# Three one-pass products for the local attention's projections, and a quantised layer whose mask TensorE adds

## What is computed

```python
def local_attention(x, Wq, Wk, Wv, Wo):     # 32 heads of 16, window 128
    q, k, v = heads(x @ Wq.T), heads(x @ Wk.T), heads(x @ Wv.T)
    scores = einsum('bhnrd,bhncd->bhnrc', blocks(q), two_blocks(k)) / sqrt(16)
    probs = softmax(where(valid, scores, min))
    return heads_joined(einsum('bhnrc,bhncd->bhnrd', probs, two_blocks(v))) @ Wo.T

def quantised(x, weight, bias):             # bias: [4, 1, 512]
    x_dq = float8_e4m3(clip(x * s, -448, 448)) / s      # s = 448 / max|x|
    w_dq = ...                                          # the same of weight
    return einsum('bmk,bkn->bmn', x_dq, w_dq) + bias

x = layernorm(x + local_attention(x, ...))
x = layernorm(x + quantised(x, ctx, mask))
```

## Time and profile before

| | us |
|---|---|
| median of 3 runs | 2390.05 |
| lowest, highest run | 2386.92, 2391.8 |
| span of the profiled execution, first to last instruction | 2399.8 |
| of it the local attention, from its first to its last stretch | 987.2 to 1499.5 |
| of it the quantised layer | 1500.2 to 1564.9 |

### The profile page before, as it was taken

One profiled execution on the slowest core, in us unless ns is written; L12 is line 12 of the kernel. 1 busy time (PEld: TensorE's weight loads), 2 busy tenths in 40 slices (PEclk: granted clock), 3 DMA queues, 4 the chain that ended last, 5 costly groups with the idle time before them and its releaser, 6 DMA issues. The chain is left out here.

```text
span 2399.8 us, 30995 instructions
## 1 busy us (share of the span) xinstructions
PE 2155.6 (90%) x10708; PEld 1150.3 (48%) x10711; DVE 1360.3 (57%) x3183; ACT 799.9 (33%) x1325; POOL 680.1 (28%) x944
## 2 busy tenths in 40 slices
PE   9999979989999999889999987478888888889994
PEld 5777748754444444344444443233333333336762
DVE  5866768856212217376667674945656565445443
ACT  5554624420122121233434332523323222123333
POOL 1300015526323320333343333011113121214553
PEclk9999989979999999999999998689999999999997
DMA  7211232270177754444333420300000000066555
GB/s 261 79 36 53 88 127 75 93 287 1 58 236 244 256 172 147 132 100 94 80 84 79 96 52 1 113 3 1 2 19 2 19 28 19 18 172 163 101 98 167
DMA packets 101672, 231.31 MB, mean 96 GB/s; under 512 B 18886, under 2 KB 42614, under 8 KB 94366
## 3 DMA queue, kind: packets, MB, share of 16 engines
q1 hardware_dynamic: 78974, 187.64, 25.2%
q0 software_dynamic: 22560, 41.87, 7.9%
HBM read 170.49 MB, written 63.53 MB: 98 GB/s over the span
## 5 line engine op out<-in xcount | busy, mean ns | idle before, releaser
L2083 DVE CUSTOM_DVE_ANT_0 D_ps<-D_ps,D_mask 128x256 f32<-128x256 f32 (+1 forms) x512 | 186.8, 420 | 68.5 <-PE D_ps L1980 67.4
L1832 POOL TENSOR_SCALAR_AFFINE_SELECT D_probs<-D_probs 128x256 f32<-128x256 f32 x256 | 106.6, 422 | 284.1 <-ACT D_probs L1890 283.8
L1890 ACT ACTIVATE D_probs<-D_ps 128x512 f32<-128x512 f32 (+1 forms) x256 | 125.3, 542 | 163.9 <-PE D_ps L2002 163.9
L3082 DVE TENSOR_REDUCE F_neg_max<-F_ps 128x4 f32<-128x2048 f32 (+1 forms) x64 | 93.9, 1489 | 109.7 <-PE F_ps L2980 103.6
L2832 ACT ACTIVATE F_probs<-F_ps 128x1536 f32<-128x1536 f32 (+1 forms) x48 | 76.4, 1591 | 189.8 <-PE F_ps L2996 189.8
L1393 PE MATMUL C_ps<-C_down_shared,C_hs 128*128 128x512 f32 x256 | 115.4, 600 | 1.9 <-DVE C_hs L1560 1.9
L1381 PE MATMUL C_ps<-C_xT,C_gate_shared 128*128 128x512 f32 x256 | 115.4, 593 | 0.5 <-ACT C_xT L1256 0.5
L1381 PE MATMUL C_ps<-C_xT,C_up_shared 128*128 128x512 f32 x256 | 115.1, 592 | 0.0
L1980 PE MATMUL D_ps<-D_k_stack,D_q_stack 96*128 96x256 bf16 (+1 forms) x512 | 92.6, 266 | 8.9 <-DVE D_maxima L2083 7.3
L1230 POOL DMA_INDIRECT expert_sums<-C_y,C_of_slot x32 | 50.3, 1571 | 173.5 <-ACT C_y L1297 102.2
L2713 POOL TENSOR_SCALAR_AFFINE_SELECT F_probs<-F_probs 128x512 f32<-128x512 f32 x64 | 41.1, 654 | 181.9 <-ACT F_probs L2832 181.9
(11 more groups left out here) (549 smaller groups left out, 4878.9 us busy)
## 6 DMA issues: line engine op xcount, KB each, us to landing
C_ring<-moe_experts_dram SPq DMA_DIRECT2D x32, 1536.0 KB, 7.2
qk_parts<-D_parts SPq DMA_DIRECT2D x32, 384.0 KB, 2.5
expert_sums<-A_zeros SPq DMA_DIRECT2D x1, 8192.0 KB
C_ring<-expert_sums SPq DMA_DIRECT2D x5, 1536.0 KB, 10.0
D_q_stack<-qk_parts SPq DMA_DIRECT2D x16, 384.0 KB, 4.9
...
```

The costliest lines, as they stand in the source:

```text
L1832: last = nc.gpsimd.affine_select(now[:, :, 0:P], now[:, :, 0:P], [[0, 2], [1, P]], ALU.is_ge, 0.0, base=0, channel_multiplier=-1)
L1890: nc.scalar.activation(probs[at % 2][:, 2 * pair:2 * pair + 2, 0:w], ps[:, 4 + unit % 3, :].rearrange("p (h q) -> p h q", h=2)[:, :, 0:w], ...
L2083: last = nc.vector.tensor_tensor_reduce(now, now, mask[:, first:256], 1.0, -3e38, ALU.add, ALU.max, maxima[n % 2][:, head, t:t + 1])
L3082: last = nc.vector.tensor_reduce(neg_max[n % 2][:, :, t], ps[:, 0:GROUP, at:at + w], AX_X, ALU.max, negate=True)
```

## The change

In the attention `x`, `Wq`, `Wk` and `Wv` are each split in a high part, rounded to a one-pass format (F32R), and the rest, and a projection or value piece becomes three one-pass products, high by high, high by low and low by high: 12 instructions per job for 8. ACT casts the high parts (`keep_xT`, `high_of`), DVE subtracts the low ones (`low_xT`, `low_of`). Pieces are spread over the half-slots by a cost in us. To make room, the stacks hold three chunks, the rest of a split one buffer, and rows of v are packed at 17 per head.

In the quantised layer the clip is fused into the rounding addition, the mask is scaled, split in three bfloat16 rows and added by one more matmul per tile, and the means are taken once per batch.

```diff
@@ window_attention_layer: the plan of the fillers
+    PIECES = {"turn_x": 1, "turn_o": 1, "project": 3 * KD, "values": 3 * KD, "out": KD}
+    COST = {"turn_x": 0.44, "turn_o": 0.44, "project": 0.23, "values": 0.23, "out": 0.86}
...
-        pieces = [(kind, n, k) for kind, n in jobs_of(i) for k in range(1 if kind.startswith("turn") else KD)]
+        pieces = [(kind, n, k) for kind, n in jobs_of(i) for k in range(PIECES[kind])]
...
+        costs = [COST[piece[0]] if piece else COST["out"] for piece in pieces]
+        least = 2 * SLOTS * (COST["out"] if i >= CHUNKS else 3 * COST["project"])
+        total, spent = max(sum(costs), least), 0.0
         for at in range(2 * SLOTS):
-            many = max(len(pieces), 2 * SLOTS)
-            now = [piece for piece in pieces[at * many // (2 * SLOTS):(at + 1) * many // (2 * SLOTS)] if piece]
+            now = []
+            while pieces and (at == 2 * SLOTS - 1 or spent + costs[0] / 2 <= (at + 1) * total / (2 * SLOTS)):
+                spent += costs.pop(0)
+                now.append(pieces.pop(0))
@@ tensors
-        xT = sb("xT", [P, KD, S])
+        xT_hi, xT_lo = sb("xT_hi", [P, KD, S], F32R), sb("xT_lo", [P, KD, S], F32R)
-        rest = [sb(f"rest{j}", [P, S]) for j in (0, 1)]
-        q_stack, k_stack = sb("q_stack", [STACK + 3, HEADS, S], BF16), sb("k_stack", [STACK + 3, HEADS, S], BF16)
-        v = [sb(f"v{j}", [P, 4, HEADS, 2 * DK]) for j in (0, 1)]
+        rest = sb("rest", [P, S])
+        q_stack, k_stack = (sb(n, [STACK + 3, RING_D * HC, S], BF16) for n in ("q_stack", "k_stack"))
+        v = [sb(f"v{j}", [P, 4, V_ROW]) for j in (0, 1)]
...
+        evicted = {"turn_x": xT_lo_ready, "project": rest_ready, "values": v_ready, "turn_o": oT_ready, "out": summed}
@@ SyncE
             def restack(m):
+                n, c = m // 2, m // 2 % RING_D
+                if n >= RING_D:
+                    sp.wait_ge(scoresT_ready, 2 * SLOTS * (n - RING_D + 1))
@@ ScalarE
+            for n in range(4):
+                keep_xT(n)
+            for k in range(KD):
+                high_of(wq_hi[:, k, :], wq[:, k, :], wq_in[k], wq_hi_ready)
+            high_of(wk_hi[:], wk[:], wk_in, wk_hi_ready)
...
+                if i == FIRST + 1:
+                    high_of(wv_hi[:], wv[:], wv_in, wv_hi_ready)
@@ TensorE, a piece of a projection (values alike)
+                    part, q = divmod(k, KD)
...
+                    if k == KD:
+                        pe.wait_ge(xT_lo_ready, 4 * (n // 8 + 1))
+                    if k == 2 * KD:
+                        pe.wait_ge(wk_lo_ready if n % 2 else wq_lo_ready, 1)
-                    last = nc.tensor.matmul(ps[:, bank, :], w[:, k, c * P:(c + 1) * P], xT[:, k, :], start=(k == 0), stop=(k == KD - 1))
+                    last = nc.tensor.matmul(ps[:, bank, :], (w_lo if part == 2 else w_hi)[:, q, c * P:(c + 1) * P],
+                                            (xT_lo if part == 1 else xT_hi)[:, q, :], start=(k == 0), stop=(k == 3 * KD - 1))
@@ VectorE
             def split(m):
-                if m >= 2:
-                    dve.wait_ge(mid_ready, m - 1)
+                if m >= 1:
+                    dve.wait_ge(lo_ready, m)
...
+            def low_xT(n):
+                dve.wait_ge(xT_ready, n + 1)
...
+                nc.vector.tensor_tensor(xT_lo[:, :, now], ps[:, number["turn_x", n] % 2, :].rearrange("p (k m) -> p k m", k=KD),
+                                        xT_hi[:, :, now].bitcast(F32), ALU.subtract).then_inc(xT_lo_ready, 1)
+            def low_of(w_lo, w, w_hi, w_hi_ready, count, w_lo_ready):
+                dve.wait_ge(w_hi_ready, count)
+                nc.vector.tensor_tensor(w_lo, w[:], w_hi[:].bitcast(F32), ALU.subtract).then_inc(w_lo_ready, 1)
...
+                        for kind, n in done(i, at, 0, "turn_x"):
+                            if n >= 4:
+                                low_xT(n)
@@ fp8_layer, SyncE
-            for b in range(B):
-                sp.dma_start(mask[:, b, :], d["mask"][b].partition_broadcast(P)).then_inc(mask_in, 16)
+            sp.dma_start(mask[:], d["mask"]).then_inc(mask_in, 16)
...
+            for z, part_ready in enumerate((mask_hi_ready, mask_mid_ready, mask_lo_ready)):
+                sp.wait_ge(part_ready, 1)
+                sp.dma_start(mask_rows[z:z + 32 * (B - 1) + 1:32, :], mask_parts[z][:]).then_inc(mask_stacked, 16)
             load_constants(sp)
@@ ScalarE
             def deviations(b):
+                act.wait_ge(mean_ready, b + 1)
                 for t in range(b * 4, b * 4 + 4):
-                    act.wait_ge(mean_ready, t + 1)
@@ TensorE
+                    nc.tensor.matmul(ps[:, t, :], ones[32 * b:32 * b + 3, :], mask_rows[32 * b:32 * b + 3, :], start=False,
+                                     stop=True).then_inc(out_ready, 1)
@@ VectorE
-                steps.after(nc.vector.tensor_scalar(w[:], w[:], FP8_MAX, -FP8_MAX, ALU.min, ALU.max))
...
-                steps.after(nc.vector.tensor_tensor(w[:], w[:], g[:], ALU.add))
+                steps.after(nc.vector.scalar_tensor_tensor(out=w[:], in0=w[:], scalar=FP8_MAX, in1=g[:], op0=ALU.min, op1=ALU.add))
...
-            def add_mask(b):
...
-                    dve.wait_ge(summed, t + 1)
-                    nc.vector.tensor_scalar(minus_mean[:, t:t + 1], sums[:, t:t + 1], -1.0 / D, None, ALU.mult).then_inc(mean_ready, 1)
+                dve.wait_ge(summed, b * 4 + 4)
+                nc.vector.tensor_scalar(minus_mean[:, b * 4:b * 4 + 4], sums[:, b * 4:b * 4 + 4], -1.0 / D, None, ALU.mult).then_inc(mean_ready, 1)
```

More of the change, by code:

```diff
@@ L2017, in times_v @@
                 for h in range(4):
+                    first = (c * HC + 4 * g + h) * (DK + 1)
                     last = nc.tensor.matmul(ps[h * (P // 4):(h + 1) * (P // 4), 7, kb * P:kb * P + w],
-                                            v[b % 2][:, kb, c * HC + 4 * g + h, :], probs[at % 2][:, h, 0:w], start=(kb == 0), stop=True,
+                                            v[b % 2][:, kb, first:first + 2 * DK], probs[at % 2][:, h, 0:w], start=(kb == 0), stop=True,
                                             skip_group_check=True)
@@ L2182, in fp8_layer @@
         minus_mean, variance, rstd = late
-        mask = sb("mask", [P, B, D])
+        mask, mask_rest = sb("mask", [B, D]), sb("mask_rest", [B, D])
+        mask_parts, mask_rows, ones = [sb(f"mask_part{z}", [B, D], BF16) for z in range(3)], sb("mask_rows", [P, D], BF16), sb("ones", [P, P], BF16)
         wq, xq = sb("wq", [P, B, KD, D], BF16), [sb(f"xq{j}", [P, 4, D], BF16) for j in (0, 1)]
@@ L2218, in _ @@
             steps = Steps(pool, pool_step)
+            nc.gpsimd.memset(ones[:], 1.0).then_inc(ones_ready, 1)
             steps.after(nc.gpsimd.memset(power[:], -0.5))
@@ L2267, in _ @@
             scale_rows(0)
+            act.wait_ge(mask_scaled, 1)
+            nc.scalar.copy(mask_parts[0][:], mask[:]).then_inc(mask_hi_ready, 1)
             scale_rows(1)
+            act.wait_ge(mask_rest_ready, 1)
+            nc.scalar.copy(mask_parts[1][:], mask_rest[:]).then_inc(mask_mid_ready, 1)
             keep_turned(0)
@@ L2318, in _, with rest_of_mask, low_of_mask @@
             dve.wait_ge(scale_ready, 1)
-            steps.after(nc.vector.tensor_tensor(inverse[:], scale[:], c_scale[:], ALU.mult))
-            steps.after(nc.vector.reciprocal(inverse[:], inverse[:]))
+            steps.after(nc.vector.tensor_tensor(both[:], scale[:], c_scale[:], ALU.mult))
+            steps.after(nc.vector.reciprocal(inverse[:], both[:]))
+            dve.wait_ge(mask_in, 16)
+            nc.vector.tensor_scalar(mask[:], mask[:], both[0:B, :], None, ALU.mult).then_inc(mask_scaled, 1)
+            def rest_of_mask():
+                dve.wait_ge(mask_hi_ready, 1)
+                nc.vector.tensor_tensor(mask_rest[:], mask[:], mask_parts[0][:], ALU.subtract).then_inc(mask_rest_ready, 1)
+            def low_of_mask():
+                dve.wait_ge(mask_mid_ready, 1)
+                nc.vector.tensor_tensor(mask_parts[2][:], mask_rest[:], mask_parts[1][:], ALU.subtract).then_inc(mask_lo_ready, 1)
             def quantise(b):
@@ L2387, in _ @@
             quantise(3)
-            add_mask(3)
             add_up(2)
```

110 lines of the change are left out of this document (70 added, 40 removed).

## The result

The change takes 2379.17 us in the median of 9 runs, against 2391.76 for 9 runs of before: a ratio of 0.995, 95% interval 0.9937 to 0.9963, 12.6 us. It is faster, and inside the range, but by less than half of the 26 us forecast. The profiled execution's span is 2383.2 us, against 2399.8.

What follows compares the result with a forecast made beforehand. PE was taken to bound the attention and DVE the quantised layer. Attention 21.6 plus layer 4.4 made 26.0 us less, from 2390.05 to a forecast of 2364 us, with a range of 2349 to 2380.

Steps and rivals of the forecast that it cites:

- the 21.6: Whole attention: 21.6 us less, summed over its iterations; bounds 16 to 27.
- One job, 0.62 us less: One projection or value job on PE: twelve one-pass products take 2.81 us for 3.43, saving 0.62.
- The rival of products that cost no less: Attention's one-pass products save nothing, only the layer gains 4.4 us: 2386 us; chance 0.05.
- Four-job iterations: Iterations 2, 3, 6, 7, 10, 11: 2.1 us less each of PE's 2.5, 12.6 in all; bounds 0.6 and 2.5.
- Iterations 4, 8, 12: Two-job attention iterations with slots evened by cost: 1.4 us less each, 4.2 in all; bounds 0.3 and 2.
- Iterations 1, 5 and 9: Paired transposes delay maxima about 2 us, mostly absorbed: 0.5 us less each in 5 and 9, 0 in 1.
- The start: Before the loop's first scores 0 (bounds -2 and +3); iteration -1 gains 1.9 us, iteration 0 gains 0.9.
- Iteration 2: Attention: 2.1 us less as a four-job iteration, plus 1 us from a different handover by iteration 1 (bounds 0 and 2.1).
- The layer, 4.4 taken: Quantised layer: shifts 8.6 us earlier, less 1.5 for 20 matmuls and 2.7 for four deviations: 4.4 less; bounds 3 and 9.
- The clock rival: PE's waits in attention lower its clock, 2.1 us a fall, thirteen falls cancel the gain; 2419 us, chance 0.05.
- The sign I had set for it: Granted clock under 0.95 in the attention loop's iterations would show that PE's clock falls and the forecast is wrong.
- the rival of the waits: DVE and two maxima banks pace slots 0 to 5; four-job iterations gain 0.6 us, total 12.4: 2378 us; chance 0.15.

Runs made afterwards that it cites:

- experiment 5: Copy of a finished group (D_pv) put between the two first maxima of slots 0 and 4 on DVE, against the kernel with maxima ahead of differences: 2371.75 us, one execution.
- Experiment 3: The change with DVE's xT_lo differences of a half-slot put after its maxima (the maxima first), against the change: 2374.81 us, ratio 0.992 to before.
- The attention alone: The change's attention with the quantised layer of before, against before: 2377.73 us, ratio 0.9927.
- experiment 10: Unread one-pass products filling PE's waits in iterations 0 and 1, added to the kernel with maxima first, copy between and last means per tile: 2357.55 us, ratio 0.9845 to before.

## Why the prediction was right and wrong

Between the two profiles the attention gave 7.3 us of the 21.6. Of the 14.3 that are missing, 5.3 lie in iterations 1, 5 and 9, 6.2 in the start and iteration 0, 3.0 in the six iterations of four jobs and 0.6 in 4, 8 and 12; from iteration 13 on it took 0.8 less, which I had at 0.

- **One job, 0.62 us less: right.** 0.23 us per product, and iterations of four jobs can take 24.32 us (experiment 5), 2.7 under before. The rival of products that cost no less is out.
- **Four-job iterations, 2.1 taken: 1.75 measured** in iteration 3 (27.03 to 25.28), 1.6 to 1.9 in 6, 7, 10 and 11. Of the chain I named, the maxima held nothing up in iteration 3; it was the copy of D_pv in slot 4, queued behind a split and two maxima, that kept one slot at its old length.
- **Iterations 4, 8, 12: 1.4 taken, 1.2 measured.** Right.
- **Iterations 1, 5 and 9, the step that failed.** I named the queue, cast, difference, maxima, PE, and put its delay at 2 us, but wrote "most is absorbed in the next slots" and left 0, 0.5 and 0.5 us of gain. The runs show in its place that PE, with two banks for scores, stood for each. Iteration 9, at clock 1.00 before and after, has it by itself: PE was busy 1.46 us less (27.77 for 29.23) and idle 1.55 us more (4.09 for 2.54), so the waits took the whole saving and no later slot made them up. Iteration 5 has the same waits and took 1.6 us longer than 9, at clock 0.95: a fall that I had at nothing in these iterations. Iteration 1 lost 2.5 us, with 1.1 us of waiting for maxima and its first two slots at 0.59 and 0.80; there the queue and the clock are not shown apart, and with the maxima first it still took from 27.6 to 33.2. Together 1, 5 and 9 lost 4.3 us (29.65 + 33.44 + 31.86 against 27.13 + 31.79 + 31.77). Experiment 3 gives 30.5 for 5 and 9, a gain of 1.3 each over before, from moving three lines.
- **The start, the other step that failed.** I took 1.9 us of gain in iteration -1 and 0 ahead of it (and read 43.79 of 49.60 as the time ahead, a row that holds iteration -1 too; ahead of it PE was busy 25.91 of 29.58). Both profiles of the change lost over 3, other builds with the same start nothing to 2. The saving on PE ahead of the loop became a longer wait for the stack of keys (2.8 us for 1.4), as I had written for the time ahead; but after it the clock is at 0.86, where before it was 1.00. The attention alone, with the same instructions, kept 1.00 in iteration -1:

```profile
1019.58:1038.65 19.07, 15.70 (x81) 9.86 (x82) 14.46 (x70) 4.15 (x8) 0.00 (x0) 1.00 0.61 149
```

There 1.0 of the 1.9 arrives: PE is busy 2.2 us less, but waits 1.1 more, for maxima and their last part (1.7 and 1.5 us for 1.1 and 1.0); and the time ahead is 1.0 longer. So the start gains nothing even where iteration -1 keeps its clock, and the other 3 us of the change's go with the lower clock. Why that fell in one execution and not in another stays open.

- **Iteration 2: 3.1 taken, 1.7 measured.** The fall of the clock stayed, and so did the wait ahead of it (3.58 us for 3.45); with that wait filled, in experiment 10, the iteration took 24.3 at 1.00.
- **The layer, 4.4 taken, 4.8 measured**, and by its own steps: ACT from the shifts on, 20 matmuls in the last step, four deviations behind one mean. But the sum came out better than its terms: the shifts came 9.5 us earlier, not 8.6, the step took 9.19 us at the low clock, not 7.7, and the tail cost 1.9, not 2.7. That these misses cancel is luck.
- **The rivals.** The time came out at that of the waits, 2378, but only in part by that mechanism: PE's idle time in iteration 3 rose by 0.3 us, not 1.5. The clock rival was priced about rightly (2.1 us a fall; 2.0 in experiment 10, 1.6 between iterations 5 and 9) and came to a few falls more, not thirteen: iterations -1, 0, 1 and 5 ran at 0.86, 0.86, 0.86 and 0.95, before at 1.00, 0.93, 0.96 and 1.00. The sign I had set for it, a clock under 0.95 in the loop's iterations, was met in -1 to 2 (0 and 2 were under it before, too). The median lies inside the range, near its upper end, only because that was drawn to take in the rival of the waits.

The Trainium skill, page TensorE: Matmul & The Clock Gate, section A second HAM failure mode: psum-queue depth-cycling, says that short pauses between groups can bring the clock down again and again. The runs agree in part: with pauses of 1.81 and 1.27 us iteration 5 was at 0.95 in the change, iteration 9, with the same pauses, at 1.00.
